# A fused attention and feed-forward layer on one core: two normalisations change engines, and all orders with them

## The reference

```python
x = layernorm(x + attention(x))          # linear attention, 16 heads of 16
x = layernorm(x + ffn(x))

def ffn(x):
    h = layer_norm(x, ln1_g, ln1_b)
    h = h @ ternary(w1).T + b1           # 256 -> 1024
    h = gelu(h)                          # exact
    h = layer_norm(h, ln2_g, ln2_b)      # over 1024
    return h @ ternary(w2).T + b2        # 1024 -> 256
```

## Time and profile before

| | us |
|---|---|
| median of the runs shown | 689.72 |
| profiled execution, its time | 687.29 |
| its span, first to last instruction | 685.5 |
| TensorE / VectorE / ScalarE / GpSimd busy in the span | 575.0 / 529.7 / 484.5 / 416.5 |

### The profile page before, as it was taken

One profiled execution on the slowest core, in us unless ns is written; L12 is line 12 of the kernel. 1 busy time (PEld: TensorE's weight loads), 2 busy tenths in 40 slices (PEclk: granted clock), 3 DMA queues, 4 the chain that ended last, 5 costly groups with the idle time before them and its releaser, 6 DMA issues. The chain is left out here.

```text
span 685.5 us, 11287 instructions
## 1 busy us (share of the span) xinstructions
PE 575.0 (84%) x3674; PEld 516.5 (75%) x3674; DVE 529.7 (77%) x1302; ACT 484.5 (71%) x902; POOL 416.5 (61%) x391
## 2 busy tenths in 40 slices
PE   2789898988899898959382589999999999999981
PEld 2678888888898788949272488888888888888871
DVE  3985797887969687765563358999899999999886
ACT  1261557575664747474626498999999999999983
POOL 0377686949678686845202256666666666666661
PEclk9999999999999999979677599999999999999996
DMA  7301003040302203330002300022222211200002
GB/s 275 132 1 61 1 25 161 1 184 2 153 31 93 91 1 123 124 124 1 31 31 96 121 32 31 1 63 63 63 62 63 63 62 62 63 32 32 33 32 92
DMA packets 10705, 46.45 MB, mean 68 GB/s; under 512 B 1312, under 2 KB 1568, under 8 KB 8352
## 3 DMA queue, kind: packets, MB, share of 16 engines
q1 hardware_dynamic: 10656, 45.83, 18.4%
HBM read 29.02 MB, written 16.81 MB: 67 GB/s over the span
## 5 line engine op out<-in xcount | busy, mean ns | idle before, releaser
L1438 PE MATMUL yps<-ff_w,ff_a_hi 128*128 128x258 f32 x512 | 126.0, 282 | 0.9 <-DVE ff_a_lo L1238 0.7
L1438 PE MATMUL yps<-ff_w,ff_a_lo 128*128 128x258 f32 x512 | 125.9, 282 | 0.0
L1422 PE MATMUL hps<-ff_ht_hi,x_hi_then_t 128*128 128x512 f32 x256 | 106.5, 416 | 3.1 <-DVE ff_a_lo L1238 2.7
L1238 DVE SCALAR_TENSOR_TENSOR ff_a_lo<-hps,ff_rho,ff_a_hi 128x512 fp32r<-128x512 f32 x128 | 93.9, 743 | 14.7 <-ACT ff_a_hi L1155 12.5
L1422 PE MATMUL hps<-ff_ht_lo,x_hi_then_t 128*128 128x512 f32 x256 | 102.3, 399 | 0.0
L1141 ACT ACTIVATE hps<-hps,bias,wstep 128x512 f32<-128x512 f32 x128 | 95.5, 775 | 9.3 <-PE hps L1422 8.7
L1438 PEld LDWEIGHTS yps<-ff_w,ff_a_hi 128*128 128x128 f32 x512 | 96.9, 189 | 4.7 <-ACT ff_a_hi L1155 0.9
L1438 PEld LDWEIGHTS yps<-ff_w,ff_a_lo 128*128 128x128 f32 x512 | 96.7, 189 | 3.3
L1155 ACT ACTIVATE ff_a_hi<-hps,ff_rho 128x512 fp32r<-128x512 f32 x128 | 92.4, 722 | 0.0
L1113 POOL TENSOR_TENSOR ff_accp<-ff_accp,ff_sq 128x512 f32<-128x512 f32 x64 | 83.3, 1301 | 7.1 <-ACT ff_sq L1153 3.5
L1153 ACT ACTIVATE ff_sq<-hps 128x512 f32<-128x512 f32 x128 | 79.7, 623 | 0.1
(11 more groups left out here) (193 smaller groups left out, 1762.3 us busy)
## 6 DMA issues: line engine op xcount, KB each, us to landing
x_scratch<-z SPq DMA_DIRECT2D x16, 514.0 KB, 2.8
ff_x<-x_scratch SPq DMA_DIRECT2D x16, 514.0 KB, 4.9
xc<-in_x_chan_dram SPq DMA_DIRECT2D x8, 1024.0 KB, 6.5
xt<-in_x_tok_dram SPq DMA_DIRECT2D x8, 1024.0 KB, 4.8
out_dram<-ff_z SPq DMA_DIRECT2D x16, 512.0 KB, 3.3
xc<-in_w_dram SPq DMA_DIRECT2D x1, 1024.0 KB, 4.9
qw<-in_w_dram SPq DMA_DIRECT2D x1, 1024.0 KB, 7.0
rows<-in_rows_dram SPq DMA_DIRECT2D x1, 512.0 KB, 4.8
```

The lines of the kernel that those rows point to most:

```text
L1238: nc.vector.scalar_tensor_tensor(out=a_lo[:, m % DEPTH], in0=ring(k, m), scalar=rho[:, m:m + 1], in1=a_hi[:, m % DEPTH].bitcast(F32), op0= ...
L1422: mm = nc.tensor.matmul(ring(k, m), t1[:, c, m * P:(m + 1) * P], h[:, k % 2, c], start=(c == 0 and j == 0), stop=(c == CH - 1 and j == 1))
L1438: last = nc.tensor.matmul(yps[:, t, 0:C + 2], a[:, m % DEPTH, t * P:(t + 1) * P], w2[:, m], start=(m == 0 and j == 0), stop=(m == FC - 1 a ...
```

## The change

ScalarE did `normalise_out` and VectorE `norm_apply`; now VectorE does `normalise_out`, as one tensor_scalar (multiply, add) for each 128x256, and ScalarE does `norm_apply`, as a Copy with a scale. The loops of all four engines get another order, and the ring another sequence (`FIRST_AT`, `HT_AT`, `SUM_AT`, the waits in `transposes`, `sum_transposes` and `first`). `out_shift` no longer waits for `o_ok`, since the same engine now both makes and uses `nmr`. The work in sum is the same.

```diff
-    FIRST_AT = (-1, 0, 1, 3, 5, 6, 7, 8)
-    HT_AT = (-13, -9)
-    SUM_AT = 15
+    FIRST_AT = (-2, 0, 1, 3, 4, 6, 7, 8)
+    HT_AT = (-12, -9)
+    SUM_AT = 16
 # GpSimd, for k in range(-1, NK + 4):
-                square_sum(k - 3, 5)
-                keep_residual(k - 2, 0)
                 square_sum(k - 2, 1)
                 keep_residual(k - 2, 1)
                 square_sum(k - 2, 2)
                 square_sum(k - 2, 3)
+                square_sum(k - 2, 4)
                 hidden_rstd(k - 3)
-                square_sum(k - 2, 4)
+                square_sum(k - 2, 5)
                 out_rstd(k - 4)
                 norm_rstd(k + 1)
+                keep_residual(k - 1, 0)
 # ScalarE
+            def norm_apply(k, ts):
+                act.wait_ge(n_rstd, k + 1)
+                wait_for(act, ht_tr, CH * k)
+                for t in ts:
+                    nc.scalar.activation(xn[:, t], x1[:, k % XB, t, 0:C], ACT.Copy, scale=rs1[:, t:t + 1]
+                                         ).then_inc(n_ok, 1)
+            for k in range(-1, NK + 1):
+                gelu(k - 1, 2)
+                ht_high(k, 1)
+                square_and_high(k - 1, 2)
+                gelu(k - 1, 3)
+                gelu(k - 1, 4)
+                square_and_high(k - 1, 3)
+                square_and_high(k - 1, 4)
+                norm_apply(k + 1, (0, 1))
+                gelu(k - 1, 5)
+                gelu(k - 1, 6)
+                square_and_high(k - 1, 5)
+                gelu(k - 1, 7)
+                square_and_high(k - 1, 6)
+                norm_apply(k + 1, (2, 3))
+                square_and_high(k - 1, 7)
+                gelu(k, 0)
+                ht_high(k + 1, 0)
+                gelu(k, 1)
+                square_and_high(k, 0)
+                square_and_high(k, 1)
 # VectorE
+            def normalise_out(k, ts):
+                dve.wait_ge(z_nmr, k + 1)
+                for t in ts:
+                    nc.vector.tensor_scalar(z[:, k % 2, t], z[:, k % 2, t], rsZ[:, t:t + 1], nmr[:, t:t + 1],
+                                            ALU.mult, ALU.add).then_inc(o_ok, 1)
+            for k in range(-1, NK + 3):
+                square_total(k - 1)
+                residual(k - 2, (2, 3))
+                ht_low(k + 1, 0)
+                act_low(k, 0)
+                hidden_mean(k - 1)
+                centre_y(k - 1, (0, 1))
+                act_low(k, 1)
+                centre_y(k - 1, (2, 3))
+                ht_low(k + 1, 1)
+                act_low(k, 2)
+                normalise_out(k - 3, (0, 1))
+                out_stats(k - 2, (0, 1))
+                act_low(k, 3)
+                act_low(k, 4)
+                hidden_stats(k - 1)
+                normalise_out(k - 3, (2, 3))
+                out_stats(k - 2, (2, 3))
+                act_low(k, 5)
+                out_variance(k - 2)
+                residual_gain(k - 1)
+                act_low(k, 6)
+                out_shift(k - 2)
+                residual(k - 1, (0, 1))
+                square_sum(k, 7)
+                act_low(k, 7)
 # TensorE: transposes
                 if c == 0:
-                    if k >= 2:
-                        bank_free(k - 2, 4)
+                    if 1 <= k < 2:
+                        pe.wait_ge(ht_lo_ok, CH * (k - 1) + 2)
+                    elif k >= NK - 14:
+                        bank_free(k - 2, 5)
                 else:
-                    pe.wait_ge(ht_lo_ok, CH * k + 1)
+                    if k >= 1:
+                        bank_free(k - 1, 0)
 # sum_transposes
-                    bank_free(k + 1, 1)
+                    bank_free(k + 1, 2)
 # first: what m waits for, after the fill
-        m = 0: bank_free(k - 1, 5)                 m = 3: bank_free(k, 0)
-        m = 4: bank_free(k, 2)                     m = 7: r_sum, k
+        m = 0: r_sum, k - 1                        m = 3: ht_lo_ok, CH * (k + 1) + 1
+        m = 4: bank_free(k, 1)                     m = 7: bank_free(k, 4)
 # TensorE, for k in range(-2, NK + 1):
-                second(k - 1, 5)
                 first(k, 1)
-                first(k, 2)
                 second(k - 1, 6)
                 second(k - 1, 7)
+                first(k, 2)
                 transposes(k + 1, 1)
                 first(k, 3)
-                sum_transposes(k - 1)
                 first(k, 4)
                 second(k, 0)
+                second(k, 1)
+                sum_transposes(k - 1)
                 first(k, 5)
                 first(k, 6)
-                second(k, 1)
                 first(k, 7)
                 second(k, 2)
                 second(k, 3)
-                transposes(k + 2, 0)
                 first(k + 1, 0)
                 second(k, 4)
+                second(k, 5)
+                transposes(k + 2, 0)
```

More of the change, by code:

```diff
@@ L1161, in _ @@
                                      scale=g_hi[:, m:m + 1].bitcast(F32)).then_inc(w2_ok, 1)
-            def normalise_out(k, ts):
+            def norm_apply(k, ts):
                 if not 0 <= k < NK:
                     return
-                act.wait_ge(z_nmr, k + 1)
+                act.wait_ge(n_rstd, k + 1)
+                wait_for(act, ht_tr, CH * k)
                 for t in ts:
-                    nc.scalar.activation(z[:, k % 2, t], z[:, k % 2, t], ACT.Identity, bias=nmr[:, t:t + 1],
-                                         scale=rsZ[:, t:t + 1]).then_inc(o_ok, 1)
+                    nc.scalar.activation(xn[:, t], x1[:, k % XB, t, 0:C], ACT.Copy, scale=rs1[:, t:t + 1]
+                                         ).then_inc(n_ok, 1)
             act.wait_ge(g_step, 6)
-            for k in range(-1, NK + 3):
+            for k in range(-1, NK + 1):
[3 more added lines that the diff above has]
+                gelu(k - 1, 3)
                 gelu(k - 1, 4)
+                square_and_high(k - 1, 3)
+                square_and_high(k - 1, 4)
+                norm_apply(k + 1, (0, 1))
                 gelu(k - 1, 5)
-                square_and_high(k - 1, 4)
+                gelu(k - 1, 6)
                 square_and_high(k - 1, 5)
-                gelu(k - 1, 6)
                 gelu(k - 1, 7)
                 square_and_high(k - 1, 6)
-                ht_high(k + 1, 0)
+                norm_apply(k + 1, (2, 3))
                 square_and_high(k - 1, 7)
                 gelu(k, 0)
-                normalise_out(k - 3, (0, 1))
+                ht_high(k + 1, 0)
+                gelu(k, 1)
                 square_and_high(k, 0)
-                gelu(k, 1)
-                gelu(k, 2)
                 square_and_high(k, 1)
-                square_and_high(k, 2)
-                gelu(k, 3)
-                ht_high(k + 1, 1)
-                square_and_high(k, 3)
-                normalise_out(k - 3, (2, 3))
         @block.vector
@@ L1215, in split_gain @@
                                         ).then_inc(s_ok, 1)
-            def norm_apply(k, ts):
-                if not 0 <= k < NK:
-                    return
-                dve.wait_ge(n_rstd, k + 1)
-                wait_for(dve, ht_tr, CH * k)
-                for t in ts:
-                    nc.vector.tensor_scalar(xn[:, t], x1[:, k % XB, t, 0:C], rs1[:, t:t + 1], None, ALU.mult
-                                            ).then_inc(n_ok, 1)
             def ht_low(k, c):
@@ L1323, in out_shift @@
                 dve.wait_ge(z_rstd, k + 1)
-                wait_for(dve, o_ok, TB * k)
                 nc.vector.scalar_tensor_tensor(out=nmr[:], in0=mvZ[:, :, 0], scalar=-1.0, in1=rsZ[:],
                                                op0=ALU.mult, op1=ALU.mult).then_inc(z_nmr, 1)
-            split_gain()
-            for k in range(-3, NK + 2):
+            def normalise_out(k, ts):
+                if not 0 <= k < NK:
+                    return
+                dve.wait_ge(z_nmr, k + 1)
+                for t in ts:
+                    nc.vector.tensor_scalar(z[:, k % 2, t], z[:, k % 2, t], rsZ[:, t:t + 1], nmr[:, t:t + 1],
+                                            ALU.mult, ALU.add).then_inc(o_ok, 1)
+            split_gain()
+            for k in range(-1, NK + 3):
[15 more added lines that the diff above has]
+                normalise_out(k - 3, (2, 3))
                 out_stats(k - 2, (2, 3))
-                act_low(k, 4)
+                act_low(k, 5)
                 out_variance(k - 2)
                 residual_gain(k - 1)
-                act_low(k, 5)
-                residual(k - 1, (0, 1))
-                out_stats(k - 1, (0, 1))
                 act_low(k, 6)
                 out_shift(k - 2)
+                residual(k - 1, (0, 1))
                 square_sum(k, 7)
                 act_low(k, 7)
-                square_total(k)
-                residual(k - 1, (2, 3))
-                ht_low(k + 2, 0)
-                act_low(k + 1, 0)
-                hidden_mean(k)
-                centre_y(k, (0, 1))
-                act_low(k + 1, 1)
-                act_low(k + 1, 2)
-                centre_y(k, (2, 3))
```

(14 more changed lines are left out.)

16 lines of the change are left out of this document (7 added, 9 removed).

## The result

The change makes the kernel slightly slower. Over 17 executions of each, the new kernel has a median of 691.65 us and the old one 688.72: ratio 1.0052 [1.0037, 1.0066]. Forecast were 682 us and a range of 676 to 690; sign and range were both missed.

A forecast was written before the change was run, and what follows sets the result against it. TensorE and ScalarE were nearly full, with a loop of waits through hidden_mean and VectorE closing the 17.44 us period. Steady -8.0, fill -3.1 and tail +3.3 gave -7.8; applied to the 689.72 median, 682 us, range 676 to 690.

The forecast's parts named there:

- I then walked the other waits at 16.9: Hand check of ScalarE, PSUM bank and GpSimd waits at a 16.9 us period: tight places worth 0 to 0.3.
- The steady term: Over 15 feed-forward periods, the period falls from 17.44 to 16.9 us: -8.0 us, bounds -14 and 0.
- the loop through hidden_mean: Old loop from second(k-1,7) via hidden_mean, centre_y, act_low(k,1) to sum_transposes: 2.09 through VectorE plus 15.35 on TensorE; to be opened.
- The wait of TensorE forecast before transposes(k+1, 1): New wait of TensorE for act_low(k,0): about 0.12 us, plus a restart of 0.28.
- The durations: Step estimates: norm_apply on ScalarE 0.40 us each, normalise_out on VectorE 0.32 us each.
- The fill: Start of the feed-forward half: first(0,4) starts near 393.0 instead of 396.2, -3.1 us, bounds 0 and -4.
- the two waits that were to go: In the fill: transposes(0,1) for ht_low(0,0), 1.71 us idle, and first(0,4) for act_low(0,2), 2.51 idle.
- The tail: End of the kernel: VectorE's added normalise_out, out_stats and out_shift's wait for GpSimd, less savings: +3.3 us, bounds +2 and +5.
- Rival 2: VectorE's normalise_out stands behind GpSimd's sums: period 18.1, +10 us in total, 700 us; chance 0.10.
- Rival 4: VectorE reaches act_low(k,0) late, so the order does nothing: period near 17.4, time 689 or 690 us; chance 0.10.
- Rival 3: Tight places restart TensorE or norm_apply costs 0.495: period 17.1 to 17.4, total -2, 688 us; chance 0.17.
- Rival 1: TensorE's restart and wait vanish or tight places do not bite: period 16.5 to 16.75, -12, 677 us; chance 0.18.

The follow-up runs named there:

- Experiment 1: The changed kernel with three z buffers and three store semaphores instead of two, nothing else: 680.45 us, ratio 0.9885 to the kernel before.
- experiment 2: The changed kernel, two z buffers, the wait for the store moved from the end of residual_gain to the head of residual: 682.39 us, ratio 0.9914 to before.
- experiment 8: The changed kernel, two z buffers, each 512 KB store issued as two of 256 KB: 687.91 us, ratio 1.0007 to the kernel before.
- experiment 9: The changed kernel, two z buffers, SyncE's load held back until the chunk's first residual, after the store has landed: 686.27 us, ratio 0.9991 to before.
- experiment 3: The kernel before the change with a third z buffer, nothing else: 687.54 us, ratio 0.9997 to the kernel before.
- experiment 6: The changed kernel with three z buffers and second(k-1, 5) moved behind first(k, 1) on TensorE: 682.55 us, ratio 0.9927 to the kernel before.
- experiment 7: The changed kernel, two z buffers, SyncE issuing the load ahead of the store: 691.41 us, ratio 1.0049 to the kernel before.
- experiment 10: The kernel before with norm_apply and normalise_out swapped between VectorE and ScalarE, old order and ring kept: 705.33 us, ratio 1.0277 to the kernel before.
- experiment 11: The changed kernel with three z buffers and steps around first(k, 2) reordered on TensorE, VectorE and ScalarE: 678.57 us, ratio 0.9873 to the kernel before.
- experiment 12: The changed kernel, three z buffers, steps around first(k, 2) reordered, norm_apply(k+1, (2, 3)) ahead of gelu(k-1, 7): 683.58 us, ratio 0.9933 to before.
- experiment 5: The changed kernel's order with the old engines, three z buffers and two buffers for rsZ and nmr: 679.69 us, ratio 0.9885 to the kernel before.

## Why the prediction was wrong

**The step that failed** is one sentence: "I then walked the other waits at 16.9". The walk followed the waits for banks of PSUM on every engine and for GpSimd's sums. It left out the one wait of VectorE for a transfer, `o_out` at the end of residual_gain, and so put it at nothing. All it needed was in the trace of before and in the diff: a store that takes 3.3 to 3.5 us with a load behind it, and about 2 us of steps on VectorE between normalise_out(k-3, (2, 3)) and residual_gain(k-1). It would have given some 1.5 us of wait per period. Measured are 1.4 to 1.8 in eight of the 13, 2.4 in one (its store took 4.3) and 0.7 to 0.9 in the last four, which have no load. Experiment 1 takes away this wait and nothing else, and the steady part falls from 263.79 to 254.44 us. Experiments 2, 8 and 9 shrink it in three other ways, and the time follows; experiment 3 shows that a third buffer gives the kernel before nothing. For the steady part this is shown, not argued. (The 1.8 of the tail and the 0.8 of the fill are other matters, below.)

A wait of 1.69 does not lengthen its period by as much (that period is 17.94, so by 1.0): with three buffers VectorE stands 0.45 at the same place for a_hi, and 0.3 at another.

**The steady term** (-8.0) was right in mechanism: the loop through hidden_mean is open, and without the store's wait a period is 16.97 where 16.9 was forecast, -7.2 over 15. The wait of TensorE forecast before transposes(k+1, 1) was 0.12, and 1.66 for the pair behind it with the restart. In the change the wait is 0.59, since act_low is late. In experiment 1 the timeline of PE shows the forecast size, by starts:

```profile
512.55 0.39 PE L1427 MATMUL hps<-ff_ht_lo,x_hi_then_t 128*128 128x512 f32 x1
512.90 0.63 PE L1374 MATMUL hps<-ident,ff_xn 128*128 128x128 f32 x4
...
514.55 0.47 PE L1427 MATMUL hps<-ff_ht_hi,x_hi_then_t 128*128 128x512 f32 x1
```

From the last product of first(k, 2) to transposes is 0.35, where a product otherwise steps by 0.23, so a wait of 0.12; from transposes to first(k, 4) it is 1.65. In experiment 6 the two are 0.24 (no wait) and 1.42, so the restart is 0.23 where 0.28 was put. That it refills the queue of weights is a reason that no run here tests.

**The durations** were right. norm_apply on ScalarE steps by 0.40 (two in 0.80), normalise_out on VectorE by 0.33 (two in 0.65), against 0.40 and 0.32:

```profile
520.97 0.97 ACT L1168 ACTIVATE ff_xn<-ff_x,ff_rs 128x256 f32<-128x256 f32 x2
521.77 1.48 ACT L1141 ACTIVATE hps<-hps,bias,wstep 128x512 f32<-128x512 f32 x2
```

The groups of normalise_out and out_shift, ns min/median/max:

```profile
L1324 DVE TENSOR_SCALAR ff_z<-ff_z,ff_rsZ,ff_nmr x64: 396/406/1511, 446.2 to 686.7; 128x256 f32<-128x256 f32 x64
```
```profile
L1316 DVE SCALAR_TENSOR_TENSOR ff_nmr<-ff_mvZ,ff_rsZ x16: 150/152/164, 437.4 to 685.5; 128x4 f32<-128x4 f32 x16
```

out_shift, 0.52 in the earlier trace rows, takes 0.15 and at most 0.16, as the new place behind GpSimd's pow was to give.

**The fill** (-3.1) came to -2.4 here and to -3.2 in experiment 1, whose code is the same up to the first store. The size held, though not every part: the two waits that were to go are gone, but a new one for act_low(0, 0) came, which the forecast did not name, and one for ht_low (1.65) moved ahead of first(0, 0). What parts the two fills is the clock. In this trace TensorE waits for act_low(0, 0):

```profile
390.66 0.85 PE L1374 MATMUL hps<-ident,ff_xn 128*128 128x128 f32 x4 [1.87 <-DVE ff_a_lo L1230]
...
393.01 0.63 PE L1427 MATMUL hps<-ff_ht_hi,x_hi_then_t 128*128 128x512 f32 x1
```
```profile
388.00:391.00 3.00, 1.13 (x7) 0.67 (x6) 0.92 (x2) 3.00 (x6) 0.70 (x1) 0.99 0.00 0
391.00:394.30 3.30, 3.30 (x11) 2.63 (x10) 2.08 (x3) 2.90 (x5) 2.90 (x3) 0.50 0.11 27
```

The columns of the second fence are those of the earlier trace rows; the granted clock follows POOL. Behind the wait it is 0.50 (1.2 GHz) over these 3.3 us, and a product of 512 columns steps by 0.43 instead of 0.23. In experiment 1 the same wait is 1.61 and the clock stays at 1.00:

```profile
394.10 0.63 PE L1374 MATMUL hps<-ident,ff_xn 128*128 128x128 f32 x4 [1.61 <-DVE ff_a_lo L1230]
```

From there to first(0,4) it takes 1.39 us, against 2.35 here: 0.96 for the clock. Experiments 2 and 7 fell to the lower clock as well, behind a wait of 1.88 and 1.87; 8 and 9 did not, behind 1.47 and 1.61; all have the same instructions in the fill. The clock had first risen to 1.00 some 0.9 us earlier in those that fell, so TensorE was done sooner and waited longer. Why it rises earlier in some executions is open.

The cost is not one of the profiled execution alone. The mean clock is 0.939 to 0.942 in 8 of the 17 executions of the change and 0.944 to 0.946 in the others, with medians of 692.0 and 691.5 us; of the 19 executions of the kernel before that went with experiments 9 to 12, none is below 0.942 and two are at it. So the fall may be some 0.3 us of the +2.9 in the medians. Only the profiled executions show where in the span the clock fell.

**The tail** (+3.3, bounds +2 and +5) came to +5.7, and to +3.9 with three z buffers. From the last hidden_mean to the last out_shift it is 4.5 longer than before, and 4.2 in experiment 1, where 3.9 was forecast. Forecast terms held: the last out_shift waits openly for GpSimd (1.12), and the last four normalise_out take 1.38. The store, once more, holds VectorE for 0.69 and 1.42:

```profile
679.45 0.16 DVE L1316 SCALAR_TENSOR_TENSOR ff_nmr<-ff_mvZ,ff_rsZ 128x4 f32<-128x4 f32 x1 [1.42 <-DMA out_dram<-ff_z]
...
685.54 0.16 DVE L1316 SCALAR_TENSOR_TENSOR ff_nmr<-ff_mvZ,ff_rsZ 128x4 f32<-128x4 f32 x1 [1.12 <-POOL ff_rsZ L1091]
685.74 1.38 DVE L1324 TENSOR_SCALAR ff_z<-ff_z,ff_rsZ,ff_nmr 128x256 f32<-128x256 f32 x4
```

But these waits mostly cover others. In experiment 1 the same two steps wait 0.45 for a_hi and, as forecast, 1.09 for GpSimd's pow:

```profile
670.77 0.16 DVE L1316 SCALAR_TENSOR_TENSOR ff_nmr<-ff_mvZ,ff_rsZ 128x4 f32<-128x4 f32 x1 [1.09 <-POOL ff_rsZ L1091]
```

So the store accounts for 0.24 and 0.33 of the 1.8 between the two tails. The rest, some 1.2, is one meeting with GpSimd at the beginning of the last chunk; VectorE here, then GpSimd, then VectorE at the same place in experiment 1, which loses 0.4:

```profile
658.01 2.80 DVE L1324 TENSOR_SCALAR ff_z<-ff_z,ff_rsZ,ff_nmr 128x256 f32<-128x256 f32 x2
```
```profile
657.94 4.14 POOL L1113 TENSOR_TENSOR ff_accp<-ff_accp,ff_sq 128x512 f32<-128x512 f32 x3
```
```profile
651.14 1.15 DVE L1324 TENSOR_SCALAR ff_z<-ff_z,ff_rsZ,ff_nmr 128x256 f32<-128x256 f32 x2
```

Counted from first(15,4), residual_gain is 1.25 later here than in experiment 1, ahead of both waits.

**The rivals.** Rival 2 (normalise_out meets GpSimd's sums) has the right sign and is right as a mechanism, but it happens once: 29 of the 30 other groups of normalise_out in the trace are pairs of 0.72 or 0.73, the last is the group of four at 685.74. Here VectorE issued 0.07 us behind GpSimd and the pair took 2.72 by steps instead of 0.65. The rule of the Trainium skill in SBUF — State Buffer, "Who interferes with whom", by which the second to issue is blocked, agrees; the loss at this meeting is 2.1 us of VectorE's time, against 0.4 in experiment 1. Rival 4 (VectorE reaches act_low(k, 0) late) comes nearest to what happened, VectorE late at the end of its round, but gave another reason, out_shift's stall, and stopped at no change. Rival 3 had the steady time at 17.1 to 17.4; it was 17.6 in the mean (263.79 / 15), beyond it. Rival 1 is what experiment 11 reaches (16.74), by another order; its 677 should read 678 by its own sum (689.7 - 12), which changes nothing.

## What to carry to other kernels

When an operation changes engine, list every buffer that it reads or writes last, and for each the wait of whoever takes the buffer next; then compare the time from release to that wait with the duration of what lies between, a store included. Place the wait for a buffer directly ahead of the instruction that needs it: moved by one step, waits of 18.7 us in all shrank to 2.4 (experiment 2). When an order and an engine change together, run each alone, with the buffers it needs: here the order held the gain without the swap (experiment 5), and the swap in the old order left the period as it was until the first store (experiment 10).

## What the runs showed of the hardware

A store of 512 KB lands later when a load of 514 KB is issued 0.4 to 0.8 us behind it on the same queue. In the trace of the change the nine stores with a load behind them take 3.3 to 4.3 us, median 3.5, and those behind the last load, with nothing after them, 2.6 each. With the load held back (experiment 9) the nine take 2.6 to 3.3, median 2.7, and the load, too, falls from a median of 4.9 to 3.7. I had taken a transfer's duration as a property of the transfer. SBUF — State Buffer in the Trainium skill, "The DMA setup-cost knee", has a fit, 2 us and the bytes at 436 GB/s, which makes an estimate of 3.2 for this store; the trace lies 0.3 above it with a load behind, and 0.6 below for the one alone.

One and the same wait of TensorE in the fill was followed by 3.3 us at half the granted clock where it lasted 1.87 us, and by none where it lasted 1.61. The fill, with the same instructions, thus differs by 0.8 us between the traces of the change and of experiment 1, more than some terms of the sum.
